# Attention and feed-forward kernel: scores of a pair of heads by 64-row tiles in two PSUM banks

## The chip, the cores and the metric

The kernel runs on one core of one Trainium2 chip. The metric is the device time of one execution in microseconds; lower is better.

## The reference

```python
# x: (16, 256, 128) float32
xn = layernorm(x)                                    # no scale, no shift
# attention: 16 heads of 8 dimensions
q = (xn @ Wq + bq);  latent = xn @ Wl + bl           # latent: 32 wide
k = latent @ Wk + bk;  v = latent @ Wv + bv          # each reshaped to (B, S, 16, 8)
scores = einsum('bihd,bjhd->bhij', q, k) * 8 ** -0.5
attn = softmax(scores, axis=-1)
a = einsum('bhij,bjhd->bihd', attn, v).reshape(B, S, 128) @ Wo + bo
# feed-forward: product keys, 8 heads, query of 2 x 16, 32 keys on each side
f = xn @ fWq + fbq                                   # (B, S, 8, 32), batch norm over it
s0, s1 = scores of the normalised halves against the two sets of normalised keys
top 4 of each side, the 16 sums of them, softmax -> w; the index of a sum picks an expert
eh = gelu(down[idx] . xn) * w;  m = sum of up[idx] * eh
out = x + a + m
```

## The kernel before, in words

The 16 sequences of 256 tokens make T = 4096 tokens. A first stage handles them in 8 chunks of 512 tokens (NC = 8): layer norm on DVE and ACT, transposes on PE, and the projections. Each of q and k is split into three bfloat16 parts (`parts`), spilled to DRAM (`spill`, on SP's queue) and read back (`load`) into QS and KS, in an order that makes one matmul over 48 rows (6 products of parts x 8 dimensions, `ROWS`) the exact score of one head. Head e of a pair (e = 0, 1) lies on partitions 64*e to 64*e+47, and rows 64*e+48 and 49 of QS take minus the row maximum of each query in two parts (`max_rows`, four DMAs per sequence) against rows of ones in KS. QS has one copy for each head of a pair: in the copy of head e the rows of the other head are zero, so a matmul over all 128 rows sees one head alone. The zeros and the ones are written by POOL at the very start, with a memset of QS (`qzero`) and one of KS (`kone`); SP waits for both before the first spill.

The main stage has 128 slots, one for each pair of heads of each sequence (n = 8*b + pr), and a further 17 slots in which the pipeline empties. A sequence, eight slots, is called a batch here, and k = slot % 8. The order of the work on each engine is written out by hand as a loop over slots, and the engines meet only through semaphores:

- PE in slot s: `si`, the scores of pair s with queries on partitions, two matmuls for each head (L506, bf16, 256 columns each), one PSUM bank for each head; `SJ`, the transposed scores minus the maximum of pair s-11 (LAG = 11), four matmuls over 128 rows (L565) into one of two 1024-wide buffers; in even slots or odd ones the product of exponentials and values (L587). From slot 10 on, head 0 of `si` stands ahead of SJ and head 1 behind it. In slots 1 to 9 both heads are issued together.
- DVE in slot s: the row maximum of each head, one 512-wide reduction for each (L844), which frees the bank for the next slot.
- ACT in slot s: the exponential of a whole SJ buffer (L404), and copies out of PSUM.
- Around these, by k, stands the feed-forward part of the batch: at k=0 DVE splits the maxima into two bf16 parts (L825, L827, `mpart`), and PE transposes them (L599); at k=1 and 2 PE makes the key scores (L611, called fs), ACT copies them, and DVE takes the top 8 at k=2 and 3 (L867, MAX8); POOL works from k=4 on a chain of small operations on them that ends with two large products (L1016) and one sum (L1024) at k=6 and 7; PE multiplies with these at k=3 (L627), collects the attention output at k=5 (L638), transposes it at k=6 (L645) and makes the output at k=7 (L652, L653).

The lines at the start that the prediction speaks of: L718 and L722 (layer norm statistics), L725 (variance plus epsilon, a TENSOR_SCALAR on 128x4) and L711 (normalising, TENSOR_SCALAR on 128x128) on DVE, L446 (the first transposes) on PE, which also waits for the constants and for fWq (L219), and L915 to L919 (the memsets) on POOL. L941, in slot 8 on POOL, adds the output bias to all of x. L549, on PE in slot 11, and L855, on DVE in slot 12, turn norms.

## Time and profile before

| | us |
|---|---|
| median of 3 runs | 505.98 |
| the three runs | 506.55, 505.98, 501.67 |
| span of the profiled execution | 500.5 |

The span goes from the first to the last instruction of one profiled execution. Which of the three runs was profiled isn't told; what lies around the span is between 1.2 and 6.1 us. Engines are PE (TensorE matmul), PEld (its weight loads), DVE (VectorE), ACT (ScalarE), POOL (GpSimd) and SP (the queue that issues the DMAs, SPq). Matmuls are pipelined and their ends are modelled: a matmul of 107 ns of streaming shows a duration of some 280 ns, and overlapping ones are merged in a timeline, so the step from one start to the next tells what a group costs. PEclk is the granted TensorE clock, 1.00 for 2.4 GHz and 0.50 for 1.2 GHz.

### The profile page before, as it was taken

The page shows a single profiled execution, that of the slowest core. Times are in us where ns is not written, and L with a number is a line of the kernel's source. Part 1 is how long each engine was busy: PE and PEld are TensorE (multiplying, and loading weights), DVE is VectorE, ACT ScalarE, POOL GpSimd, SP SyncE. Part 2 cuts the span into 40 slices and gives each one's busy share as a digit, 9 for nine tenths or more (in the row PEclk, how much of TensorE's full clock was granted, in tenths as well). Part 3 has the DMA queues.
Part 4 walks back from the last instruction along what each step waited for, and adds up shares of the span by engine and source line. Part 5 has one row for each costly group of instructions (what it writes and reads, how often), then busy time and mean ns, then how long its engine had stood idle before and what let it go on. Part 6 is the DMA issues. An engine that isn't in the chain of part 4 may idle for free.

```text
span 500.5 us, 10238 instructions
## 1 busy us (share of the span) xinstructions
PE 430.4 (86%) x3276; PEld 247.5 (49%) x3276; DVE 419.2 (84%) x1622; ACT 257.2 (51%) x387; POOL 291.3 (58%) x495
## 2 busy tenths in 40 slices
PE   0488768865799999999999999999999999999886
PEld 0353434331336465555556464656555564646554
DVE  6958659999789898888898898989888888989651
ACT  1265528761555555445555555555555555555560
POOL 9502016675295665849494756658494947566670
PEclk9999959996669999898999999999989899999997
DMA  7100583542814031231402040312304030000000
GB/s 208 23 1 1 114 107 96 136 127 55 105 24 65 15 52 47 32 63 15 75 2 77 3 76 22 55 49 29 68 9 75 3 77 3 10 14 1 24 0 22
DMA packets 45821, 24.79 MB, mean 50 GB/s; under 512 B 5384, under 2 KB 45640, under 8 KB 45768
## 3 DMA queue, kind: packets, MB, share of 16 engines
q1 hardware_dynamic: 45768, 24.14, 24.5%
q8 instruction: 26, 0.43, 0.4%
q14 instruction: 27, 0.22, 0.2%
HBM read 15.47 MB, written 8.39 MB: 48 GB/s over the span
## 4 chain that ended last, share of the span: by engine, by line
PE 57%; DVE 15%; issue 3%; POOL 3%; DMA 1%; POOLq 1%; SPq 0%; ACT 0%; DVEq 0%
PE bank L506 13%; PE SJ L565 11%; PE bank L587 9%; PE bank L611 6%; PE bank L627 6%; PE bank L638 5%; DVE mpart L827 4%; DVE negm L844 3%; DVE mpart L825 2%; PE bank L645 2%; DVE parts L686 2%; PE bank L652 2%; PE bank L653 1%; DVE r_sb L876 1%; DMA QS<-mT 1%
## 5 line engine op out<-in xcount | busy, mean ns | idle before, releaser
L844 DVE TENSOR_REDUCE negm<-bank 128x2 f32<-128x512 f32 x256 | 169.3, 683 | 32.2 <-PE bank L506 30.6
L404 ACT ACTIVATE Eb<-SJ 128x1024 f32<-128x1024 f32 x128 | 130.9, 1023 | 100.4 <-PE SJ L565 100.1
L506 PE MATMUL bank<-KS,QS 48*128 48x256 bf16 x512 | 99.1, 284 | 13.8 <-DVE negm L844 9.2
L565 PE MATMUL SJ<-QS,KS 128*128 128x256 bf16 x512 | 80.6, 282 | 0.4 <-DMA QS<-mT 0.4
L587 PE MATMUL bank<-Eb,vhat 128*32 128x256 f32 x1024 | 73.1, 406 | 0.0
L949 POOL COPY top<-top 128x32 f32<-128x32 f32 x32 | 6.7, 209 | 111.6 <-DVE top L867 111.6
L506 PEld LDWEIGHTS bank<-KS,QS 48*128 48x128 bf16 x512 | 27.6, 95 | 69.3 <-issue 33.4
L1016 POOL TENSOR_TENSOR prod<-r_sb,a 128x1024 f32<-128x1024 f32 x31 | 59.6, 1943 | 0.0
L565 PEld LDWEIGHTS SJ<-QS,KS 128*128 128x128 bf16 x512 | 41.1, 99 | 31.1 <-issue 26.0
L927 POOL TENSOR_TENSOR Eb<-Eb,parts 128x512 f32<-128x512 f32 x16 | 20.4, 1289 | 57.9 <-ACT parts L294 57.9
L867 DVE MAX8 top<-s_sb 128x8 f32<-128x32 f32 x512 | 50.5, 176 | 3.5 <-ACT s_sb L378 3.5
L876 DVE MATCH_REPLACE8 r_sb<-top,s_sb 128x36 f32<-128x36 f32 x256 | 42.7, 179 | 0.0
L587 PEld LDWEIGHTS bank<-Eb,vhat 128*32 128x32 f32 x1024 | 27.7, 113 | 26.9 <-issue 16.7
L611 PE MATMUL bank<-kblk,fqT 128*128 128x256 f32 x128 | 38.1, 422 | 0.1
L1024 POOL TENSOR_TENSOR prod<-prod 128x1024 f32<-128x1024 f32 x15 | 35.2, 2348 | 1.2
L627 PE MATMUL bank<-cst,prod 128*128 128x128 f32 x256 | 32.8, 281 | 2.2 <-DVE ysb L816 2.2
L387 ACT ACTIVATE Osb<-bank 128x256 f32<-128x256 f32 x64 | 24.1, 376 | 19.0 <-PE bank L587 19.0
L378 ACT ACTIVATE s_sb<-bank 128x512 f32<-128x512 f32 x32 | 19.1, 597 | 28.3 <-PE bank L611 28.3
L627 PEld LDWEIGHTS bank<-cst,prod 128*128 128x128 f32 x256 | 29.8, 191 | 5.8 <-issue 3.2
L638 PE MATMUL bank<-cst,Osb 128*128 128x36 f32 x256 | 31.5, 280 | 0.6 <-ACT Osb L387 0.6
L638 PEld LDWEIGHTS bank<-cst,Osb 128*128 128x128 f32 x256 | 29.8, 191 | 4.3 <-issue 4.3
L611 PEld LDWEIGHTS bank<-kblk,fqT 128*128 128x128 f32 x128 | 22.7, 197 | 12.3 <-issue 9.5
(149 smaller groups left out, 671.5 us busy)
## 6 DMA issues: line engine op xcount, KB each, us to landing
qk_parts<-parts SPq DMA_DIRECT2D x48, 128.0 KB, 2.4
QS<-qk_parts SPq DMA_DIRECT2D x32, 96.0 KB
KS<-qk_parts SPq DMA_DIRECT2D x32, 96.0 KB
x_sb<-L_attn_x SPq DMA_DIRECT2D x8, 256.0 KB, 3.7
QS<-qk_parts SPq DMA_DIRECT2D x32, 64.0 KB
KS<-qk_parts SPq DMA_DIRECT2D x32, 64.0 KB
out<-ysb SPq DMA_DIRECT2D x16, 128.0 KB, 3.9
QS<-qk_parts SPq DMA_DIRECT2D x32, 32.0 KB
```

Source lines behind the costliest of these rows:

```text
L404: A(Eb[:, n % 4, :], SJ[n % 2][:, :], ACT.Exp).then_inc(s["ex"], 1)
L506: last = mm(SI[e][:, t * S:(t + 1) * S], QS[r, b % RING, e, pr, t * P:(t + 1) * P], KS[r, b % RING, pr, :], start=True, stop=True)
L565: last = mm(SJ[n % 2][:, (e * BT + t) * S:(e * BT + t + 1) * S], KS[:, b % RING, pr, t * P:(t + 1) * P], QS[:, b % RING, e, pr, :], start= ...
L587: last = mm(psO[32 * c:32 * c + 32, (g % 2) * S:(g % 2 + 1) * S], vhat[:, v0:v0 + 32], Eb[:, (2 * g + c // 2) % 4, e0:e0 + S], start=(t == ...
L611: last = mm(psM[:, 256 * r:256 * (r + 1)], fqT[:, r, tok:tok + P], kblk[:, :, :].rearrange("p g k -> p (g k)"), start=True, stop=True)
L627: last = mm(psM[:, t * P:(t + 1) * P], prod[:, t, h, :, :].rearrange("p i j -> p (i j)"), ident, start=(h == 0), stop=(h == FH // 2 - 1))
L638: last = mm(ct[:, :, 2 * g * VC:2 * (g + 1) * VC], Osb[:, g, t * P:(t + 1) * P], sel, start=True, stop=True)
L844: V.tensor_reduce(negm[:, bb % 2, e, :, pr], SI[e].rearrange("p (t j) -> p t j", j=S), axis=AX, op=ALU.max, negate=True).then_inc(s["mx"], 1)
L867: last = V.max(top8[:, h, a, :], s_sb[:, h, a, 0:NK])
L876: last = V.match_replace(r_sb[:, h, :], top4[:, h, :], s_sb[:, h, 1, :], NEG)
L1016: TT(prod[:, t, :, :, :], r_sb[:, hs, 0:NK].unsqueeze(2).to_broadcast([P, FH, TOP, NK]), a0[:, hs, :].unsqueeze(3).to_broadcast([P, FH, TO ...
L1024: TT(prod[:, :, 0:FH // 2, :, :].rearrange("p t h i j -> p t (h i j)"), prod[:, :, 0:FH // 2, :, :].rearrange("p t h i j -> p t (h i j)"), ...
```

## The change

Both heads of a pair are now computed by matmuls on row tiles, head 0 on rows 0 to 47 (or 49) and head 1 on rows 64 to 111 (or 113), issued in turn (head inside, half of the queries or keys outside), and head e writes into bank e of a two-bank buffer. SI gets two such buffers; the second is used from slot 11 on (`FIRST2` = 10; up to slot 10 all slots use the first). SJ keeps one. QS has one copy, without zeros. All four matmuls of `si` stand ahead of SJ in every slot. The maxima of both heads are one 1024-wide reduction, and its semaphore counts slots and no longer heads. SJ of pair n waits for the exponential of pair n-1 (before: n-2). Both memsets are gone; the rows of ones come by two DMAs from 64 more columns of `const`, queued on SP behind the weight loads, and SP doesn't wait for them; PE does before the first SJ. PSUM buffers of the first stage are placed anew.

```diff
--- before.py
+++ after.py
@@ -30,7 +30,8 @@
 
 
 C_ID, C_SEL, C_AVG, C_GRP = 0, 128, 164, 292
-C_END = C_GRP + 248
+C_ONE = C_GRP + 248
+C_END = C_ONE + 64
 
 
 def constants():
@@ -42,6 +43,7 @@
             c[32 * col + r, C_SEL + 18 * (col % 2) + 9 * (col // 2) + r] = 1.0
     c[:, C_AVG:C_AVG + P] = (p[:, None] % 32 == p[None, :] % 32) / 8.0
     c[p, C_GRP + 120 + p // 16] = 1.0
+    c[:, C_ONE:C_END] = np.array([0x3F803F80], np.uint32).view(np.float32)
     return c
 
 
@@ -119,7 +121,7 @@
         bnv = sb("bnv", [P, 16])
         fqT = sb("fqT", [P, 2, T])
         rn_t = sb("rn_t", [P, CH]); rn = sb("rn", [P, NT, G])
-        QS = sb("QS", [P, RING, 2, NPAIR, S], BF16)
+        QS = sb("QS", [P, RING, NPAIR, S], BF16)
         KS = sb("KS", [P, RING, NPAIR, S], BF16)
         negm = sb("negm", [P, 2, 2, BT, NPAIR])
         mpart = sb("mpart", [P, BT, 2, 2, NPAIR], BF16)
@@ -146,22 +148,26 @@
         prod = sb("prod", [P, BT, FH, TOP, NK])
         wgT = sb("wgT", [P, S])
 
-        bank = [ctx.enter_context(nc.psum_tensor(f"bank{i}", [P, 512], F32)) for i in range(4)]
-        SJ = [ctx.enter_context(nc.psum_tensor(f"SJ{i}", [P, 1024], F32)) for i in range(2)]
-        SI = [bank[0][:, :], bank[1][:, :]]
-        psO, psM = bank[2][:, :], bank[3][:, :]
-
-        psX = [psO, SJ[1][:, 512:1024]]
-        psQ, psK, psV = SJ[0][:, 0:512], SJ[0][:, 512:1024], SJ[1][:, 0:512]
+        SI = [ctx.enter_context(nc.psum_tensor(f"SI{i}", [P, 1024], F32)) for i in range(2)]
+        SJ = ctx.enter_context(nc.psum_tensor("SJ", [P, 1024], F32))
+        bank = [ctx.enter_context(nc.psum_tensor(f"bank{i}", [P, 512], F32)) for i in range(2)]
+        psO, psM = bank[0][:, :], bank[1][:, :]
+
+        psX = [psO, SI[1][:, 512:1024]]
+        psQ, psK, psV = SJ[:, 0:512], SJ[:, 512:1024], SI[1][:, 0:512]
         psW = psQ
-        psF = [SI, [psM, psV]]
+        psF = [[SI[0][:, 0:512], SI[0][:, 512:1024]], [psM, psV]]
         psN = psO
-        psG = [psM, SJ[1][:, 512:1024]]
+        psG = [psM, SI[1][:, 512:1024]]
+        FIRST2 = NC + 2
+
+        def si_buffer(n):
+            return SI[n % 2] if n >= FIRST2 else SI[0]
 
 
         names = (
 
-            "w0 w w2 stats aggr var std rstd nm xn xn2 xT xnT vone kone qzero pad identb "
+            "w0 w w2 stats aggr var std rstd nm xn xn2 xT xnT vone kone pad identb "
 
             "wl wl_ev wkv wkv_ev q q_ev k k_ev v v_ev f f_ev f_st "
 
@@ -222,6 +228,11 @@
                         sp.dma_start(dst, src).then_inc(s["w"], 16)
             for dst, src in W2LOADS:
                 sp.dma_start(dst, src).then_inc(s["w2"], 16)
+            for e in range(2):
+                r0 = 64 * e + ROWS
+                ones = KS[r0:r0 + 2, :, :, :].rearrange("p a r n -> p (a r n)").bitcast(F32)
+                sp.dma_start(ones.rearrange("p (a n) -> p a n", n=64),
+                             const[0:2, C_ONE:C_END].unsqueeze(1).to_broadcast([2, RING * NPAIR * S // 128, 64])).then_inc(s["kone"], 16)
 
             def spill(c):
 
@@ -241,7 +252,7 @@
                 if b >= RING:
                     sp.wait_ge(s["sj"], NPAIR * (b - RING + 1))
                 for e in range(2):
-                    for t, dst in ((0, QS[:, b % RING, e]), (1, KS[:, b % RING])):
+                    for t, dst in ((0, QS[:, b % RING]), (1, KS[:, b % RING])):
                         for term, part, length in RUNS[t]:
                             r0 = 64 * e + DH * term
                             src = scratch[t, c, NPAIR * e:NPAIR * (e + 1), part:part + length].rearrange("r a d n -> (a d) r n")
@@ -254,10 +265,8 @@
                     for part in range(2):
                         src = (e * 2 + part) * NPAIR
                         r0 = 64 * e + ROWS + part
-                        sp.dma_start(QS[r0:r0 + 1, b % RING, e, :, :], mT[src:src + NPAIR, :]).then_inc(s["mrow"], 16)
-
-            sp.wait_ge(s["kone"], 1)
-            sp.wait_ge(s["qzero"], 1)
+                        sp.dma_start(QS[r0:r0 + 1, b % RING, :, :], mT[src:src + NPAIR, :]).then_inc(s["mrow"], 16)
+
             spill(0)
             load(0)
             load(1)
@@ -401,7 +410,7 @@
                     elif n == 0:
                         act.wait_ge(s["lo_q"], NC)
                         act.wait_ge(s["lo_k"], NC)
-                    A(Eb[:, n % 4, :], SJ[n % 2][:, :], ACT.Exp).then_inc(s["ex"], 1)
+                    A(Eb[:, n % 4, :], SJ[:, :], ACT.Exp).then_inc(s["ex"], 1)
                 if slot == NC + 2:
                     act.wait_ge(s["n2r"], NC // 2)
                     A(rn_t[:, :], rn_t[:, :], ACT.Sqrt).then_inc(s["n2s"], 1)
@@ -491,21 +500,26 @@
                 last.then_inc(s["bb"], 1)
                 pe.wait_ge(s["bc"], 1)
 
-            def si(n, heads):
+            def si(n):
 
                 b, pr = n // NPAIR, n % NPAIR
-                if pr == 0 and 0 in heads:
+                if pr == 0:
                     pe.wait_ge(s_load[b % RING], 16 * NLOAD * (b // RING + 1))
-                for e in heads:
-                    if n >= 1:
-                        pe.wait_ge(s["mx"], 2 * (n - 1) + e + 1)
-                    else:
-                        pe.wait_ge(s["f_ev"], 2 * NC)
-                    r = slice(64 * e, 64 * e + ROWS)
-                    for t in range(BT):
-                        last = mm(SI[e][:, t * S:(t + 1) * S], QS[r, b % RING, e, pr, t * P:(t + 1) * P],
-                                  KS[r, b % RING, pr, :], start=True, stop=True)
-                    last.then_inc(s["si"], 1)
+                if n == 0:
+                    pe.wait_ge(s["f_ev"], 2 * NC)
+                elif n <= FIRST2:
+                    pe.wait_ge(s["mx"], n)
+                elif n == FIRST2 + 1:
+                    pe.wait_ge(s["v_ev"], NC)
+                    pe.wait_ge(s["g_ev"], NC)
+                else:
+                    pe.wait_ge(s["mx"], n - 1)
+                for t in range(BT):
+                    for e in range(2):
+                        r = slice(64 * e, 64 * e + ROWS)
+                        last = mm(si_buffer(n)[:, (e * BT + t) * S:(e * BT + t + 1) * S],
+                                  QS[r, b % RING, pr, t * P:(t + 1) * P], KS[r, b % RING, pr, :], start=True, stop=True)
+                last.then_inc(s["si"], 1)
 
             def norms(c):
 
@@ -530,7 +544,7 @@
                     bn_mean()
                 if slot < NPAIR * B:
 
-                    si(slot, (0,) if slot > NC + 1 else (0, 1))
+                    si(slot)
                 if slot == 0:
                     bn_variance()
                 if 1 <= slot <= NC:
@@ -554,20 +568,19 @@
                     b, pr = n // NPAIR, n % NPAIR
                     if pr == 0:
                         pe.wait_ge(s["mrow"], 64 * (b + 1))
-                    if n >= 2:
-                        pe.wait_ge(s["ex"], n - 1)
+                    if n >= 1:
+                        pe.wait_ge(s["ex"], n)
                     else:
+                        pe.wait_ge(s["kone"], 32)
+                        pe.wait_ge(s["q_ev"], NC)
                         pe.wait_ge(s["k_ev"], NC)
-                        pe.wait_ge(s["v_ev"], NC)
-                        pe.wait_ge(s["g_ev"], NC)
-                    for e in range(2):
-                        for t in range(BT):
-                            last = mm(SJ[n % 2][:, (e * BT + t) * S:(e * BT + t + 1) * S],
-                                      KS[:, b % RING, pr, t * P:(t + 1) * P],
-                                      QS[:, b % RING, e, pr, :], start=True, stop=True)
+                    for t in range(BT):
+                        for e in range(2):
+                            r = slice(64 * e, 64 * e + ROWS + 2)
+                            last = mm(SJ[:, (e * BT + t) * S:(e * BT + t + 1) * S],
+                                      KS[r, b % RING, pr, t * P:(t + 1) * P],
+                                      QS[r, b % RING, pr, :], start=True, stop=True)
                     last.then_inc(s["sj"], 1)
-                if NC + 1 < slot < NPAIR * B:
-                    si(slot, (1,))
                 m = slot - LAG - 3
                 if m >= 0 and m % 2 == 0 and m // 2 < 4 * B:
 
@@ -818,7 +831,7 @@
                 b = slot // 8 - 1
                 if k == 0 and 0 <= b < B:
 
-                    dve.wait_ge(s["mx"], 2 * NPAIR * (b + 1))
+                    dve.wait_ge(s["mx"], NPAIR * (b + 1))
                     if b >= 1:
                         dve.wait_ge(s["mt"], b)
                     src = negm[:, b % 2, :, :, :].rearrange("p e t r -> p t e r")
@@ -839,10 +852,10 @@
                     q_ev(slot + 1)
                 if slot < NPAIR * B:
                     bb, pr = slot // NPAIR, slot % NPAIR
-                    for e in range(2):
-                        dve.wait_ge(s["si"], 2 * slot + e + 1)
-                        V.tensor_reduce(negm[:, bb % 2, e, :, pr], SI[e].rearrange("p (t j) -> p t j", j=S),
-                                        axis=AX, op=ALU.max, negate=True).then_inc(s["mx"], 1)
+                    dve.wait_ge(s["si"], slot + 1)
+                    V.tensor_reduce(negm[:, bb % 2, :, :, pr].rearrange("p e t -> p (e t)"),
+                                    si_buffer(slot)[:, :].rearrange("p (t j) -> p t j", j=S),
+                                    axis=AX, op=ALU.max, negate=True).then_inc(s["mx"], 1)
                 if 1 <= slot < NC - 1:
                     k_ev(slot + 1)
                 if 1 <= slot < NC:
@@ -913,8 +926,6 @@
             V = nc.gpsimd
             TT = V.tensor_tensor
             V.memset(vhat[:, :], 1.0).then_inc(s["vone"], 1)
-            V.memset(QS[:, :, :, :, :].rearrange("p c e r n -> p (c e r n)").bitcast(mybir.dt.uint32), 0).then_inc(s["qzero"], 1)
-            V.memset(KS[:, :, :, :].rearrange("p a r n -> p (a r n)"), 1.0).then_inc(s["kone"], 1)
             V.memset(s_sb[:, :, :, NK:KP], NEG)
             V.memset(top4[:, :, TOP:8], NEG).then_inc(s["pad"], 1)
 

```

## Rows read from the trace of the kernel before

**Rows 1.** The page, part 5: the costliest groups.

```profile
L844 DVE TENSOR_REDUCE negm<-bank 128x2 f32<-128x512 f32 x256 | 169.3, 683 | 32.2 <-PE bank L506 30.6
L404 ACT ACTIVATE Eb<-SJ 128x1024 f32<-128x1024 f32 x128 | 130.9, 1023 | 100.4 <-PE SJ L565 100.1
...
L587 PE MATMUL bank<-Eb,vhat 128*32 128x256 f32 x1024 | 73.1, 406 | 0.0
```

**Rows 2.** Timeline, first 21 us: start, duration, engine, line, count [idle before].

```profile
2.30 0.43 SPq L219 DMA_DIRECT2D fwq_sb<-L_ffn_Wq  x1
...
4.62 6.93 POOL L916 MEMSET QS<- 128x8192 uint32 x1
...
4.95 6.62 DVE L725 TENSOR_SCALAR ve<-mv 128x4 f32<-128x4 f32 x1
...
11.48 6.95 POOL L917 MEMSET KS<- 128x8192 bf16 x1
...
12.13 6.44 DVE L711 TENSOR_SCALAR Eb<-x_sb,mv,rs 128x128 f32<-128x128 f32 x2
...
18.72 2.05 PE L446 MATMUL bank<-cst,Eb 128*128 128x128 f32 x8 [18.72 <-DVE Eb L711]
...
19.80 0.17 DVE L725 TENSOR_SCALAR ve<-mv 128x4 f32<-128x4 f32 x1
...
20.53 0.59 DVE L711 TENSOR_SCALAR Eb<-x_sb,mv,rs 128x128 f32<-128x128 f32 x2
```

**Rows 3.** DMA issues of the first 20 us: size, us to landing.

```profile
fwq_sb<-L_ffn_Wq SPq DMA_DIRECT2D x1, 128.0 KB, 4.8
```

**Rows 4.** Timeline of PE, slot 3, both heads issued together.

```profile
78.55 0.40 PE L506 MATMUL bank<-KS,QS 48*128 48x256 bf16 x4
```

**Rows 5.** Timeline of PE in one steady batch, and L599 of the last.

```profile
283.67 0.29 PE L599 MATMUL bank<-ident_b,mpart 128*32 128x128 bf16 x2 [0.90 <-DVE mpart L827]
...
285.46 1.13 PE L611 MATMUL bank<-kblk,fqT 128*128 128x256 f32 x4
...
289.77 0.39 PE L506 MATMUL bank<-KS,QS 48*128 48x256 bf16 x2
290.09 0.61 PE L565 MATMUL SJ<-QS,KS 128*128 128x256 bf16 x4
...
290.95 2.05 PE L627 MATMUL bank<-cst,prod 128*128 128x128 f32 x16
...
466.83 0.28 PE L599 MATMUL bank<-ident_b,mpart 128*32 128x128 bf16 x2 [1.66 <-DVE mpart L827]
```

**Rows 6.** The tile negm: ns min/median/max, first and last start.

```profile
L827 DVE TENSOR_TENSOR mpart<-negm,mpart x14: 191/1845/1849, 167.2 to 464.9; 128x32 bf16<-128x32 f32 x14
```

**Rows 7.** Timeline of DVE and POOL around one steady batch.

```profile
283.54 1.87 DVE L844 TENSOR_REDUCE negm<-bank 128x2 f32<-128x512 f32 x3
...
291.67 1.57 DVE L867 MAX8 top<-s_sb 128x8 f32<-128x32 f32 x16
...
302.60 3.78 POOL L1016 TENSOR_TENSOR prod<-r_sb,a 128x1024 f32<-128x1024 f32 x2
...
303.76 0.78 DVE L825 CAST mpart<-negm 128x32 bf16<-128x32 f32 x1
...
304.58 1.85 DVE L827 TENSOR_TENSOR mpart<-negm,mpart 128x32 bf16<-128x32 f32 x1
```

**Rows 8.** Timeline of PE and DVE between slots 8 and 11.

```profile
122.34 2.07 PE L611 MATMUL bank<-kblk,fqT 128*128 128x256 f32 x4
...
131.15 0.69 DVE L844 TENSOR_REDUCE negm<-bank 128x2 f32<-128x512 f32 x1 [2.70 <-PE bank L506]
```

**Rows 9.** Windows: length, busy us by engine (count), PEclk, DMA share, GB/s.

```profile
131.70:135.10 3.40, 1.71 (x12) 0.64 (x10) 3.40 (x23) 1.18 (x2) 0.21 (x1) 1.00 1.00 100
135.10:145.30 10.20, 8.18 (x50) 2.88 (x52) 8.88 (x45) 5.07 (x6) 9.08 (x24) 0.50 0.46 54
148.00:205.00 57.00, 54.54 (x458) 31.84 (x457) 51.62 (x236) 30.89 (x43) 35.95 (x72) 1.00 0.28 46
```

## The prediction, made before the change was run

> **What bounds the kernel now.** I read the page first, then the timeline of the first 20 us, then one steady batch (eight slots) engine by engine, and last the granted clock of stretches. The page says that the maxima on DVE sat 30.6 us in all behind the score matmuls [rows 1], and in a steady stretch of 57 us PE was busy 54.5 [rows 9]. Shares don't say where an end is set, so the run is taken in parts.
>
> *The first 20 us* belong to POOL. Its memset of QS (6.93 us) and the one of KS (6.95 us) run back to back, and two small DVE operations last exactly until each ends: L725 takes 6.62 us where its next execution takes 0.17, and the pair at L711 takes 6.44 us where the next pair takes 0.59. The first matmul starts at 18.72 only because it waits for L711 [rows 2].
>
> *The steady part* is 14 batches; L827 runs once in each, 13 intervals from 167.2 to 464.9 us, so a batch takes 22.90 us [rows 6]. PE is the engine that never rests: in slot k=3 the order is scores of head 0 at 289.77, transposed scores at 290.09, head 1 behind them, next work at 290.95, which makes 1.18 us per slot for this block; it idles 0.90 us once, in front of L599 [rows 5]. A second limit lies just under it. L825 and L827, on 128x32 elements, take 0.78 and 1.85 us, and L827 ends at 306.43, with POOL's two products (302.60 + 3.78 = 306.38); I read this as DVE and POOL excluding one another. From the end of the second MAX8 group (291.67 + 1.57 = 293.24) to the end of L827 (306.43) is 13.2 us, stretch A, nearly all of it a chain of POOL operations. From the first maximum behind L827 (283.54) to 293.24 is 9.7 us, stretch B, which PE sets [rows 7]. A + B is the batch.
>
> *Between them*, slots 8 to 16, DVE once waits 2.70 us for the second head's scores, which stand behind transposed scores and other work in PE's order [rows 8].
>
> **The change part by part.**
>
> *Memsets gone.* DVE gains 6.62 - 0.17 = 6.45 us and 6.44 - 0.59 = 5.85 us, 12.3 us in a row [rows 2]. What is late next: the first matmul also waits for fWq, issued at 2.30 and landing 4.8 us later, at 7.1 us [rows 2, 3]; that would leave 18.72 - 7.2 = 11.5 us. The later chunks hang on DVE and ACT more than on this one start. Ends 11.5 and 12.3; I take 12.0. Everything behind is a chain on the same chunks, so the shift is kept to the end. The waits on kone and qzero leave SP; two DMAs that write the ones are queued on SP behind all weight loads, some 0.5 us of issue each as for other loads there, long before the first spill needs the queue: nothing. Their cost if that cover were gone is that 1 us.
>
> *Row tiles.* The trace has this operation already: in the early slots, where both heads are issued together, four L506 matmuls last 0.40 us [rows 4], while two of one head last 0.39 [rows 5]. The two heads run side by side. So scores and transposed scores, eight matmuls in four rounds of 0.11 us, need 0.44 us plus about 0.11 for the turn to other work: 0.55 us in place of 1.18. Ends: 0.55, and 0.98 if the second set (50 rows) did not overlap. I take 0.55, the near row. PE's work per batch falls by 8 x 0.63 = 5.0 us. The Trainium skill (TensorEngine Tiling (Array Packing), Tiling Modes, Key Properties) says that a change of tiling mode drains TensorE; both sets are now of one mode, and with a drain between them all the same the block would be 0.66 us, 0.9 us more per batch.
>
> *One maximum of 1024.* Three maxima in a row take 1.87 us, 0.62 each [rows 7]; two hold two fixed parts, the new one holds one. Between 1.13 (one fixed part of some 0.09 us less) and 1.25 us; I take 1.18, so 0.5 us less per batch. With two SI buffers the maximum no longer waits behind PE's slot.
>
> *SJ with one buffer.* Transposed scores now wait for the exponential of the slot before. That loop is 1.02 us of ACT [rows 1], 0.22 of matmuls and three hand-overs, taken at 0.2 each: 1.9 us, under a slot's 2.6 (an eighth of 21). In PE's queue behind the wait stand the value matmuls (L587), the feed-forward groups and the next slot's scores, for which DVE waits. Ends 0 and 0.4 us per slot (3.2 per batch); I take 0, since 1.9 is under 2.6.
>
> *Stretch B.* DVE's own work is four maxima (4.7 us) and two MAX8 groups (3.1): 7.9 us. PE's path is L599 0.4 (0.29 and a wait), block 0.55, L611 1.06 (a 1.13 us row with 0.07 of tail), block 0.55, the values 1.0 (73.1 us over 64 groups is 1.14 [rows 1], with tail), L611 1.06, scores 0.3, then one maximum and one MAX8 group: 7.7 us. So B is 7.9 where the clock is full.
>
> *Stretch A* does not shrink. DVE gains some 0.3 us in it (four maxima at 0.06), but POOL's chain is as long as before, and L825 and L827 wait for POOL's products again: 13.2. The batch would be 21.1 us.
>
> *But the clock.* PE's work is now 22.9 - 0.9 - 0.3 - 5.0 = 16.7 us in a batch of 21.1. Stretch B leaves it nearly no pause, so most of the 4.4 us left falls in A, over 3 of them in front of L599, which waits for L827; it idled 0.90 there before [rows 5]. The granted clock was 1.00 (2.4 GHz) over 57 us in which PE was busy 54.5; in the stretch from 131.7 to 135.1 PE was busy 1.71 of 3.4 us, and the 10.2 us behind it were granted 0.50 (1.2 GHz) [rows 9]. I expect this at the head of each batch, just where PE's path decides B. The fs block then takes 2.07 us in place of 1.06 [rows 5, 8]. Half clock for 3.4 us costs that path 1.7 us: 7.7 + 1.7 = 9.4. If it holds for 6.8 us it is 3.4 of the 5 us of PE's part: 11.1. Ends 7.9 and 11.1; part of a slow stretch falls into the idle time, so I take the middle, 9.5. The batch is 22.7 us, 0.2 less than now: 14 x 0.2 = 3 us. The Trainium skill (TensorE: Matmul & The Clock Gate, Part 1) says that throttled is the default and activity releases it; by that rule as by rows 9 a faster PE that must wait is punished for it.
>
> *Slots 8 to 16.* The 2.70 us wait goes, since both heads stand ahead of the transposed scores; PE is at half clock there in both. Ends 0 and 2.9; I take 2.5. POOL's long addition in slot 8 stays.
>
> *Tail.* No maxima are left, POOL's chain sets it: 0.
>
> *Sum.* 12.0 + 2.5 + 3 = 17.5 us. The profiled execution has a span of 500.5; the runs shown are 501.67 to 506.55, so between 1 and 6 us lie around it, and I cannot say which run it was. The steps are differences, so they are set against the median: 505.98 - 17.5 = 488.
>
> **The rivals.**
>
> *The clock holds* (or the slow stretches fall where PE has slack). For: before the last L599 PE idled 1.66 us [rows 5] and ran on at 2.4 GHz. Against: 3.3 us is twice that. Batch 21.1: 505.98 - 14.5 - 14 x 1.8 = 466.
>
> *DVE gets in first.* L825 starts at 303.76, 1.16 us behind POOL's products [rows 7]. Some 0.4 of that is a wait for PE's output, 0.2 one for the second head at k=7, and the shorter maxima give 0.3: about 0.25 is left, within the error of my count. If it gets in, one product (1.9 us) [rows 7] no longer stands between it and L827, A is 11.3 and the idle time of PE is about 1.5 us. Batch 19.2 to 20.9, so 28 to 52 us more than the head's gain: 440 to 463, 455 as its figure. Against: both chains start with the same MAX8 end, and nothing makes POOL's longer.
>
> *Slower: PE stays at half clock.* If PE falls at the start of each batch and the single SJ buffer keeps it too thinly fed to recover, B goes to 11.1 and A, where PE's 12 us become about 20, grows as well. The place is L611 in slots k=1 and 2, then L627 and L638. At 11.1 + 13.2 = 24.3 the loss is 14 x 1.4 = 20 us, more than the 14.5 gained before; with 0.5 more in A it is 513. It decides from a batch of 22.90 + 14.5/14 = 23.9 us. Against: slow stretches in the trace end when PE has had a full load.
>
> *It doesn't do what it says:* the head's 12 us are taken up by another wait (loads, the spill queue), or the 50-row tiles don't overlap. Then 498 to 502.
>
> **How the numbers follow.** Forecast 488 (482 to 498): 0.53. Clock holds, 466: 0.20. DVE first, 455: 0.12. Slower, 513: 0.07. Gain taken up, 500: 0.08. A measurement of this kernel tells about 1% from no change, 501 to 511 us. Faster: all of the first three and a third of the last, 0.88; within 1%: the rest of the last and an edge of the slow case, 0.06; slower 0.06. The range for 8 in 10 takes in "clock holds" and the middle of "DVE first", and leaves out most of the slow case: 455 to 501.
>
> **What would show it.** L725 at 0.17 us and the first matmul near 7 us show the head's step; anything above 9 us shows it wrong. The eight matmuls of a slot within 0.55 us show the row tiles. L844 at 1.13 to 1.25 us x128. L827 still ending with POOL's second product, 13.2 us behind the second MAX8 group, shows A; an L827 of 0.2 us would show the race won. An idle time of about 3 us before L599 with PEclk below 9 in most slices of the steady part shows the clock; PEclk at 9 throughout with a batch of 21 us, or a batch above 23.9, would make the forecast wrong.

## The result, and the profile after

The changed kernel takes 458.77 us (median of 4 runs, 454.42 to 462.76) beside 503.83 us (497.40 to 506.55) of the kernel before on the same chip: a ratio of 0.912, 95% interval 0.904 to 0.920. The ratios leave out slow runs, those over 1.5% above the fastest of their kernel, such as the 462.76 us here. By the medians it is 45 us faster, where 17.5 us were forecast. Its profiled execution has a span of 456.2 us (before 500.5), so 44.3 us are to be found. The granted clock's mean over the span is 0.929 of full, before 0.938.

The page of the kernel after, its parts 1, 2 and 5 (answering [rows 1]):

```profile
PE 357.8 (78%) x3276; PEld 219.6 (48%) x3276; DVE 402.0 (88%) x1494; ACT 254.6 (56%) x387; POOL 275.8 (60%) x493
...
PEclk9989789875689899999999999999999898999897
...
L413 ACT ACTIVATE Eb<-SJ 128x1024 f32<-128x1024 f32 x128 | 131.1, 1024 | 55.5 <-PE SJ L580 52.3
L856 DVE TENSOR_REDUCE negm<-SI 128x4 f32<-128x1024 f32 x128 | 153.7, 1209 | 9.3 <-PE SI L520 8.7
L600 PE MATMUL bank<-Eb,vhat 128*32 128x256 f32 x1024 | 72.0, 401 | 0.0
...
L612 PE MATMUL bank<-ident_b,mpart 128*32 128x128 bf16 x32 | 5.0, 242 | 45.6 <-DVE mpart L840 45.6
```

DVE now waits 8.7 us for scores in the whole run (before 30.6), and PE's largest idle time is in front of L612, 45.6 us. Half clock is rare: PEclk reads 9 through the middle of the run, which the forecast named as what would make it wrong. (Lines have moved: L725, L711, L446, L599, L611, L627, L844, L825, L827 are now L738, L724, L455, L612, L624, L640, L856, L838, L840, and L506, L565, L587, L867, L1016 are L520, L580, L600, L880, L1027.)

The timeline of its first 10 us (answering [rows 2]):

```profile
4.78 0.17 DVE L738 TENSOR_SCALAR ve<-mv 128x4 f32<-128x4 f32 x1
...
5.51 0.60 DVE L724 TENSOR_SCALAR Eb<-x_sb,mv,rs 128x128 f32<-128x128 f32 x2
...
6.75 2.07 PE L455 MATMUL bank<-cst,Eb 128*128 128x128 f32 x8 [6.75 <-DMA fwq_sb<-L_ffn_Wq]
```

L738 lasts 0.17 us where its twin lasted 6.62, and the first matmul starts at 6.75, released by the load of fWq: 12.0 us earlier.

The timeline of one steady batch, PE, DVE and POOL in turn (answering [rows 5, 7]; a number in brackets is the idle time ahead):

```profile
240.07 0.39 PE L520 MATMUL SI<-KS,QS 48*128 48x256 bf16 x4
240.30 0.38 PE L580 MATMUL SJ<-QS,KS 50*128 50x256 bf16 x4
240.61 1.07 PE L600 MATMUL bank<-Eb,vhat 128*32 128x256 f32 x16
...
253.32 0.28 PE L612 MATMUL bank<-ident_b,mpart 128*32 128x128 bf16 x2 [2.90 <-DVE mpart L840]
...
254.08 1.13 PE L624 MATMUL bank<-kblk,fqT 128*128 128x256 f32 x4
...
239.89 0.55 DVE L880 MAX8 top<-s_sb 128x8 f32<-128x32 f32 x5
...
249.89 1.50 DVE L838 CAST mpart<-negm 128x32 bf16<-128x32 f32 x1
251.42 1.84 DVE L840 TENSOR_TENSOR mpart<-negm,mpart 128x32 bf16<-128x32 f32 x1
253.19 3.62 DVE L856 TENSOR_REDUCE negm<-SI 128x4 f32<-128x1024 f32 x3
...
259.33 1.58 DVE L880 MAX8 top<-s_sb 128x8 f32<-128x32 f32 x16
...
249.44 3.78 POOL L1027 TENSOR_TENSOR prod<-r_sb,a 128x1024 f32<-128x1024 f32 x2
```

Eight score matmuls take 240.61 - 240.07 = 0.54 us, counted from their first start to the next group's. L838 starts 0.45 us behind POOL's products and L840 ends with them (253.26 beside 253.22). The second MAX8 group of the batch before (its end is the first of the DVE lines) ends at 239.89 + 0.55 = 240.44, so stretch A is 253.26 - 240.44 = 12.8 us; this batch's second group ends at 260.91, so stretch B is 7.7 us. Together 20.5.

The tile mpart of the kernel after (ns min/median/max, first and last start), answering [rows 6]:

```profile
L838 DVE CAST mpart<-negm x16: 167/1500/1582, 106.7 to 417.1; 128x32 bf16<-128x32 f32 x16
L840 DVE TENSOR_TENSOR mpart<-negm,mpart x16: 191/1843/1845, 106.9 to 418.7; 128x32 bf16<-128x32 f32 x16
```

The starts of the cast in either trace cut the run into four parts:

| part | before | after | difference | forecast |
|---|---|---|---|---|
| start to the first cast | 120.16 | 106.68 | -13.5 | -12.0 |
| first to second cast (slots 8 to 16) | 23.90 | 19.26 | -4.6 | -2.5 |
| 14 batches behind it | 320.1 | 291.2 | -28.9 | -3 |
| last cast to end | 36.4 | 39.06 | +2.7 | 0 |

So 29 of the 44 us were won where 3 had been forecast: 22.86 us per batch became 20.80. Eleven of the 14 batches take 19.95 to 20.9 us, three 22.0. A stretch at half clock starts in each of those three; the first of the 14 also catches the end of an earlier one. In the kernel before four such stretches start in its 14 batches. The mean granted clock over the 14 batches is 0.98 in both kernels.

Windows of the kernel after (length, busy us of PE, PEld, DVE, ACT and POOL with counts, PEclk, DMA share, GB/s): the pause ahead of L612 and what follows it, in a batch that takes 22.0 us, then in one that takes 20.5, then in another of 22.0, and at last the tail's slow stretch:

```profile
146.00:149.40 3.40, 0.50 (x10) 0.09 (x2) 3.37 (x3) 0.48 (x1) 3.32 (x3) 1.00 0.00 0
149.40:152.80 3.40, 3.40 (x18) 1.80 (x20) 2.12 (x2) 1.78 (x4) 2.46 (x2) 0.50 0.01 3
249.90:253.30 3.40, 0.52 (x12) 0.04 (x4) 3.37 (x4) 0.58 (x1) 3.32 (x3) 1.00 0.02 5
253.30:256.70 3.40, 3.38 (x39) 1.84 (x39) 3.35 (x3) 3.02 (x5) 2.58 (x2) 1.00 0.01 2
...
374.70:378.10 3.40, 0.53 (x12) 0.05 (x4) 3.37 (x4) 0.59 (x1) 3.33 (x2) 1.00 0.00 0
378.10:381.50 3.40, 3.37 (x16) 1.81 (x18) 2.24 (x2) 1.66 (x3) 2.58 (x2) 0.50 0.01 2
...
442.90:446.30 3.40, 3.40 (x16) 3.29 (x16) 0.00 (x0) 0.00 (x0) 0.00 (x0) 0.51 0.17 43
```

PE does the same half microsecond of work in each of the three pauses. Behind the first and the third the granted clock is 0.50 (1.2 GHz) for 3.4 us; behind the second it stays at 2.4 GHz. What decides between them these rows don't show.

### The profile page after: what moved, and what is told of

Read it like the earlier page. It is cut to its first block, busy times and chain, and to the rows that moved or that the text cites. A ratio compares the mean times of both kernels' runs of the same rounds, so it can differ in the third digit from the quotient of the medians.

```text
span 456.2 us, 10109 instructions
## 1 busy us (share of the span) xinstructions
PE 357.8 (78%) x3276; PEld 219.6 (48%) x3276; DVE 402.0 (88%) x1494; ACT 254.6 (56%) x387; POOL 275.8 (60%) x493
## 4 chain that ended last, share of the span: by engine, by line
DVE 39%; issue 15%; POOL 14%; PE 10%; POOLq 1%; DMA 1%; SPq 0%; ACT 0%; DVEq 0%
DVE negm L856 12%; DVE r_sb L889 6%; DVE top L880 6%; DVE mpart L840 4%; PE bank L624 3%; DVE mpart L838 3%; POOL prod L1035 3%; POOL prod L1027 2%; DVE parts L699 2%; PE SI L520 2%; PE bank L640 2%; POOL z_sb L977 1%; POOL rank L997 1%; DVE ysb L829 1%; POOL cmp L987 1%
## 5 line engine op out<-in xcount | busy, mean ns | idle before, releaser
L413 ACT ACTIVATE Eb<-SJ 128x1024 f32<-128x1024 f32 x128 | 131.1, 1024 | 55.5 <-PE SJ L580 52.3
L856 DVE TENSOR_REDUCE negm<-SI 128x4 f32<-128x1024 f32 x128 | 153.7, 1209 | 9.3 <-PE SI L520 8.7
L600 PE MATMUL bank<-Eb,vhat 128*32 128x256 f32 x1024 | 72.0, 401 | 0.0
L1027 POOL TENSOR_TENSOR prod<-r_sb,a 128x1024 f32<-128x1024 f32 x31 | 59.5, 1941 | 0.0
L520 PE MATMUL SI<-KS,QS 48*128 48x256 bf16 x512 | 53.3, 289 | 6.7 <-DVE negm L856 3.8
L580 PE MATMUL SJ<-QS,KS 50*128 50x256 bf16 x512 | 51.4, 280 | 5.1 <-ACT Eb L413 4.2
L880 DVE MAX8 top<-s_sb 128x8 f32<-128x32 f32 x512 | 50.4, 176 | 5.1 <-ACT s_sb L387 5.1
L624 PE MATMUL bank<-kblk,fqT 128*128 128x256 f32 x128 | 40.8, 446 | 0.3
L612 PE MATMUL bank<-ident_b,mpart 128*32 128x128 bf16 x32 | 5.0, 242 | 45.6 <-DVE mpart L840 45.6
L600 PEld LDWEIGHTS bank<-Eb,vhat 128*32 128x32 f32 x1024 | 27.4, 112 | 26.4 <-issue 16.1
L640 PE MATMUL bank<-cst,prod 128*128 128x128 f32 x256 | 34.0, 289 | 6.1 <-ACT s_sb L387 3.3
L640 PEld LDWEIGHTS bank<-cst,prod 128*128 128x128 f32 x256 | 31.3, 200 | 10.3 <-issue 6.7
L378 ACT ACTIVATE mT<-bank 32x256 bf16<-32x256 f32 x16 | 6.0, 373 | 50.2 <-PE bank L612 50.2
L387 ACT ACTIVATE s_sb<-bank 128x512 f32<-128x512 f32 x32 | 19.1, 597 | 23.7 <-PE bank L624 23.3
L520 PEld LDWEIGHTS SI<-KS,QS 48*128 48x128 bf16 x512 | 15.3, 96 | 35.4 <-issue 22.1
L624 PEld LDWEIGHTS bank<-kblk,fqT 128*128 128x128 f32 x128 | 24.1, 210 | 14.2 <-issue 8.6
```

The costliest lines, as they stand in the source:

```text
L413: A(Eb[:, n % 4, :], SJ[:, :], ACT.Exp).then_inc(s["ex"], 1)
L520: last = mm(si_buffer(n)[:, (e * BT + t) * S:(e * BT + t + 1) * S], QS[r, b % RING, pr, t * P:(t + 1) * P], KS[r, b % RING, pr, :], start= ...
L580: last = mm(SJ[:, (e * BT + t) * S:(e * BT + t + 1) * S], KS[r, b % RING, pr, t * P:(t + 1) * P], QS[r, b % RING, pr, :], start=True, stop ...
L600: last = mm(psO[32 * c:32 * c + 32, (g % 2) * S:(g % 2 + 1) * S], vhat[:, v0:v0 + 32], Eb[:, (2 * g + c // 2) % 4, e0:e0 + S], start=(t == ...
L624: last = mm(psM[:, 256 * r:256 * (r + 1)], fqT[:, r, tok:tok + P], kblk[:, :, :].rearrange("p g k -> p (g k)"), start=True, stop=True)
L640: last = mm(psM[:, t * P:(t + 1) * P], prod[:, t, h, :, :].rearrange("p i j -> p (i j)"), ident, start=(h == 0), stop=(h == FH // 2 - 1))
```

## The experiments

Theory after the result: the work itself costs 20.5 us per batch, and the clock decides how much of that is seen; PE's 2.9 us pause is a state in which it may fall. Rivals: the gain is one part of the change (second SI buffer, wide maximum, the memsets), and the clock only fills idle time.

**One part undone at a time, and one made alone.** First both memsets back on POOL, with SP waiting for them, and without the DMAs of ones.

```diff
-                sp.dma_start(ones.rearrange("p (a n) -> p a n", n=64),
...
+            V.memset(QS[:, :, :, :].rearrange("p c r n -> p (c r n)"), 0.0).then_inc(s["qzero"], 1)
+            V.memset(KS[:, :, :, :].rearrange("p a r n -> p (a r n)"), 1.0).then_inc(s["kone"], 1)
```

> The changed kernel with both memsets back on POOL at the start (8192 elements each, as long as before), SP waiting for them, and no DMAs of ones. Theory (the head's gain is two DVE operations that no longer wait for a memset, and it is kept to the end): L738 takes 6.6 us and the first L724 pair 6.4 again, the first matmul starts near 18.7 us, and the time is 12 to 13.5 us above the changed kernel, some 471 to 473 us. Rival (the head's gain is made good elsewhere, in loads or in the spill queue, and the whole gain is in the main stage): under 465 us.

Measured 483.25 us (ratio 0.948, 0.938 to 0.958), 24.5 above the changed kernel. The first cast starts at 119.09, 12.4 us later, as expected, but the time is above the expected 471 to 473. In the profiled execution (span 478.2) the other 9.6 us lie behind the first cast: 8 of its 14 batches take 21.1 to 23.4 us, the others 20.2 to 20.5. The four runs lie far apart, 475.76 to 486.45 us.

Then the kernel before with the scores of both heads ahead of SJ.

```diff
-                    si(slot, (0,) if slot > NC + 1 else (0, 1))
+                    si(slot, (0, 1))
...
-                if NC + 1 < slot < NPAIR * B:
-                    si(slot, (1,))
```

> The kernel before with one edit in PE's order: all four score matmuls stand ahead of the transposed scores in every slot, as they do up to slot 9. Still one bank for each head, 512-wide maxima, memsets, 128-row transposed scores. Theory (PE's order sets the batch): the block takes 0.33 + 0.54 = 0.87 us in place of 1.18, PE's batch is 2.5 us shorter, but head 1 now waits for its maximum ahead of the transposed scores, which gives back part: batch 21.5 to 22.4 us against 22.9, time 490 to 500 us. Rival (the second SI buffer is what pays, since the maxima's wait is the bound): no change or slower, batch 22.9 or more.

Measured 505.44 us (ratio 1.0006, 0.9972 to 1.004): nothing. Two batches without a slow stretch take 22.16 us and one 21.4, where such a batch of before takes 22.8 as a rule; the other 11 hold a slow stretch and take 23.7. So it looks as if the gain was there and the clock took it back; no run has this order with the clock held up, so that is not shown.

The changed kernel with one SI buffer, and with one SI and two SJ:

```diff
-        FIRST2 = NC + 2
+        FIRST2 = NPAIR * B
```

> The changed kernel with FIRST2 set so high that all scores go through one SI buffer of two banks. Theory (DVE and POOL set the batch now, PE has slack): each maximum waits 0.4 to 0.5 us for matmuls that can only start when the maximum before has ended; in the stretch of slots k=0 to 3 nothing hides this (1.5 us), in the POOL-bound stretch the wait of L838 for POOL's first product hides it: batch 22 us against 20.5, time 478 to 485 us. Rival (the row tiles alone bring the gain, the buffer nothing): within 3 us of the changed kernel.

> The changed kernel with the PSUM map the other way round: one two-bank buffer for the scores (SI) and two for the transposed scores (SJ), each transposed set waiting for the exponential of two slots before. Against e3 it differs by the second SJ buffer alone. Theory (one SJ buffer costs nothing, since its loop is shorter than a slot): as e3, batch 22 to 24 us, time 495 to 501 us. Rival (the single SJ buffer costs up to 0.4 us per slot): 3 us per batch less than e3, time below 470 us.

Measured 499.43 us (497.89 to 501.16) and 498.86 us (496.45 to 499.16). The first is above its expected range. With one SI buffer, a second SJ buffer is worth nothing: both have batches of 23.9 us, and both have the slow stretches. Whether it would be worth something with two SI buffers no run shows, but the trace of the changed kernel speaks against it: in its 14 batches PE never waits for an exponential in front of L580. Timeline and windows of the one-SI kernel around L612, in one batch:

```profile
291.15 0.39 PE L612 MATMUL bank<-ident_b,mpart 128*32 128x128 bf16 x2 [1.91 <-DVE mpart L840]
```

```profile
287.50:290.90 3.40, 1.61 (x24) 0.78 (x24) 3.37 (x3) 1.02 (x1) 3.40 (x2) 1.00 0.00 0
290.90:297.70 6.80, 5.81 (x38) 2.76 (x38) 4.35 (x11) 3.28 (x5) 2.71 (x3) 0.50 0.05 13
297.70:314.80 17.10, 13.57 (x152) 9.05 (x144) 16.22 (x72) 8.83 (x12) 12.03 (x27) 1.00 0.33 51
```

From the second batch on each repeats this: 6.8 us at half clock, 17.1 at full. Stretch B takes 11.1 us here, the upper end that the prediction gave it. This is its slow case, with 23.9 us per batch, its deciding point.

The changed kernel with two 512-wide maxima per slot:

```diff
+                    for e in range(2):
+                        last = V.tensor_reduce(negm[:, bb % 2, e, :, pr],
+                                               si_buffer(slot)[:, 512 * e:512 * (e + 1)].rearrange("p (t j) -> p t j", j=S),
+                                               axis=AX, op=ALU.max, negate=True)
+                    last.then_inc(s["mx"], 1)
```

> The changed kernel with two 512-wide maxima per slot (they still wait for both heads together and free the buffer together). Theory (DVE's fixed part is 0.08 us each, and DVE's path is one of two equal ones behind L840): batch up by 0.2 to 0.4 us, to 20.7 to 20.9 us, time 1 to 8 us above the changed kernel, clock falls apart. Rival (the wide maximum is a main part of the gain): more than 10 us above it.

Measured 482.16 us (480.66 to 486.02), 23 us worse: far above expectation. From the second batch on they take 22.3 or 23.6 us, with half clock in each. Each of the three undone versions lost more than was expected of the edit itself.

**The clock taken out.** Three matmuls of no use go into the pause, from the third batch on; they write a bank that the next transposes overwrite, and wait for nothing that L612's slot did not already wait for.

```diff
+                    if b >= 2:
+                        pe.wait_ge(s["fin"], b - 1)
+                        for _ in range(3):
+                            mm(psM, ident, xnT[:, 0:CH], start=True, stop=True)
                     pe.wait_ge(s["ms"], b + 1)
...
-                    if b >= 2:
-                        pe.wait_ge(s["fin"], b - 1)
```

> The changed kernel with three more matmuls per batch from the third on, fp32 128x512, results unused, on PE in the pause in front of L612 (they wait for the output sum of the batch and not for the split maxima, and end about when L840 ends). Everything else is as in the changed kernel. Theory (the pause of 2.9 us is what lets the clock fall, in some executions in many batches and in others in few, at 1.5 us or more a time): PEclk stays at 1.00 through the steady part, every batch takes 20.5 us, mean granted clock above 0.95, and the time is 449 to 455 us, with runs closer together than those of the changed kernel. Rival (the falls have another cause, such as the low activity at L651): falls stay, time 457 to 463 us. Rival (PE is late for L612 because of the extra work): batch 20.7 us or more, time above 460 us.

Measured 452.75 us (449.40 to 455.46; ratio 0.9005, 0.8963 to 0.9047), 6 us less than the changed kernel by the medians, with more work. The two intervals touch (0.9036 and 0.9047), so of this pair alone only the batches of the traces speak clearly. Its timeline of PE at the same place, and its windows, in one fence each:

```profile
267.71 2.84 PE L609 MATMUL bank<-xnT,cst 128*128 128x512 f32 x6
270.70 0.29 PE L614 MATMUL bank<-ident_b,mpart 128*32 128x128 bf16 x2 [0.15 <-DVE mpart L842]
```

```profile
267.30:270.70 3.40, 3.25 (x18) 1.06 (x7) 3.37 (x4) 0.54 (x1) 3.32 (x3) 1.00 0.00 0
270.70:274.10 3.40, 3.40 (x39) 1.86 (x39) 3.35 (x4) 3.05 (x5) 2.56 (x2) 1.00 0.04 8
```

The three matmuls (recorded as six) fill 2.84 us and the pause is down to 0.15; the clock is 1.00 from 127 to 444 us, and the batches are 20.5 us but for one of 21.3. In the changed kernel three batches were 1.5 us longer and have lost it here. The same matmuls then went into each undone version:

> The changed kernel with one SI buffer (499.43 us so far, 23.9 us per batch with half clock for 6.8 us in each), now with three idle-time fp32 matmuls of 512 columns in the pause in front of the transposes of mpart, from the third batch on; each writes a bank that the next transposes overwrite, and no result changes. Theory (the second SI buffer is worth some 1 to 1.5 us per batch by itself, the rest of the loss is the half clock that its absence brings): no half-clock stretch in the steady part, a batch of 21.5 to 22.3 us, 466 to 478 us. Rival 1 (one SI buffer costs its 3 us per batch through waits alone, the half clock is only what the waits leave behind and covers idle time): the batch stays above 23.3 us with the clock at 1.00, 490 us or more. Rival 2 (the clock is all): 20.5 to 20.8 us per batch, 452 to 457 us.

> The changed kernel with two 512-wide maxima per slot (482.16 us so far, clock falls in every batch), now with the same three matmuls in the pause. Theory (the wide maximum saves only its fixed part on DVE, 0.04 us x 8 per batch, and the rest of the 23 us that its absence cost was clock): batch 20.7 to 20.9 us, 455 to 461 us. Rival (the second maximum lengthens the hand-over from PE to DVE and back in every slot): clock at 1.00 and a batch of 21.5 us or more, over 467 us.

> The changed kernel with both memsets back on POOL (483.25 us so far), now with the same three matmuls. Theory (the memsets cost 12.4 us in the head and nothing else; the other 12 us were half-clock stretches in the steady part of those executions): 452.75 + 12.4 = 465 us, 462 to 468. Rival (the memsets, or the missing DMAs of ones, cost time in the steady part too): 475 us or more, with a batch above 21 us at a clock of 1.00.

| kernel | us | same with the three matmuls | its usual batch there | cost of the edit by itself | what the clock added |
|---|---|---|---|---|---|
| changed | 458.77 | 452.75 | 20.49 | | 6.0 |
| one SI buffer | 499.43 | 466.43 (465.13 to 468.44) | 21.52 | 13.7 | 33.0 |
| two maxima | 482.16 | 458.88 (457.21 to 461.68) | 20.80 | 6.1 | 23.3 |
| memsets | 483.25 | 465.54 (463.10 to 468.22) | 20.48 | 12.8 | 17.7 |

The cost by itself is the third column's difference from 452.75; what the clock added is the second column less the third. The memsets' 17.7 is uncertain, because of the scatter of their runs: the two shorter ones, 475.76 and 480.11, would make it 12. The groups of runs were measured apart; the kernel before took 503.08 to 503.95 us beside them. All three times and batches lie where the theories put them and the rivals fall. One SI buffer keeps two stretches at half clock in its 14 batches, so its 13.7 us may hold a little of the clock's. The page of the one-SI kernel without and with the matmuls, its row of maxima:

```profile
L856 DVE TENSOR_REDUCE negm<-SI 128x4 f32<-128x1024 f32 x128 | 155.3, 1213 | 45.0 <-PE SI L520 44.8
```

```profile
L858 DVE TENSOR_REDUCE negm<-SI 128x4 f32<-128x1024 f32 x128 | 155.1, 1212 | 16.9 <-PE SI L520 16.6
```

The same buffers, the same order: DVE's wait for scores falls from 44.8 to 16.6 us with three matmuls added, and stretch B from 11.1 to 8.7. The second SI buffer is worth 1.03 us per batch. The wide maximum is worth 0.31: two maxima of 677 ns overlap and take 1.28 us from the first start to the last end, the one takes 1.21, which is at most 0.5 us in eight slots. The rest of their 33 and 23 us came with 1.2 GHz. Between a batch of before without a slow stretch (22.81) and 20.48 there remains 1 us for the row tiles and PE's order, if the parts add up; no run undoes the row tiles alone. The same three matmuls elsewhere in the batch were not tried, so that they must stand in this pause isn't shown.

**What bounds the batch then.** DVE's maximum ahead of L838, to see whether A shortens:

```diff
-                if k == 0 and 0 <= b < B:
...
-                    V.tensor_copy(mpart[:, :, :, 0, :], src).then_inc(s["mh"], 1)
...
                                     axis=AX, op=ALU.max, negate=True).then_inc(s["mx"], 1)
+                b = slot // 8 - 1
+                if k == 0 and 0 <= b < B:
...
+                    V.tensor_copy(mpart[:, :, :, 0, :], src).then_inc(s["mh"], 1)
```

> The changed kernel with one edit in DVE's order: at k=0 the maximum of the slot stands ahead of the split of the maxima (L838, L840). Theory (L838 and L840 wait for POOL's two products whenever they are issued, while a maximum, whose input is in PSUM, does not): L840 ends with the second product as before, the maximum is done inside that wait, the stretch from there to the second MAX8 group is 1.1 us shorter, batch 19.3 to 19.5 us, time 442 to 446 us. Rival (L838 and L840 are slow by themselves, or wait for something in DVE's own queue): the batch stays at 20.5 us.

Measured 469.79 us (468.38 to 471.16): worse. Timeline of one batch, all engines:

```profile
299.30 3.78 POOL L1028 TENSOR_TENSOR prod<-r_sb,a 128x1024 f32<-128x1024 f32 x2
...
299.75 1.22 DVE L847 TENSOR_REDUCE negm<-SI 128x4 f32<-128x1024 f32 x1
300.88 0.37 DVE L857 CAST mpart<-negm 128x32 bf16<-128x32 f32 x1
301.28 1.84 DVE L859 TENSOR_TENSOR mpart<-negm,mpart 128x32 bf16<-128x32 f32 x1
...
303.18 0.28 PE L612 MATMUL bank<-ident_b,mpart 128*32 128x128 bf16 x2 [2.90 <-DVE mpart L859]
...
303.83 1.23 DVE L847 TENSOR_REDUCE negm<-SI 128x4 f32<-128x1024 f32 x1 [0.71 <-PE SI L520]
...
305.44 1.23 DVE L847 TENSOR_REDUCE negm<-SI 128x4 f32<-128x1024 f32 x1 [0.38 <-PE SI L520]
```

The maximum runs beside POOL's products at no cost, so DVE has one less to do in B; but it then waits 0.71 and 0.38 us for PE. The batch without a slow stretch stays at 20.47, and B in it at 7.65 us, so PE's path and DVE's tie there. The order also brought more slow stretches: 9 of the 14 batches take 20.9 to 23.5 us.

Transposed scores twice, with the three matmuls in the pause:

```diff
-                    for t in range(BT):
+                    for t in list(range(BT)) * 2:
```

> The changed kernel with the three matmuls in the pause (452.75 us), and each slot's four transposed-score matmuls issued twice, the second time over the same result: 0.22 us more of PE's work per slot, 1.8 us per batch. Theory (with the clock full, PE's path and DVE's tie in stretch B, and A hangs on POOL): only the slots of stretch B count, so the batch grows by 0.4 to 0.7 us, 458 to 463 us. Rival 1 (PE's order bounds every slot): plus 1.8 us per batch, 476 us or more. Rival 2 (DVE alone bounds B): no change, 451 to 455 us.

Measured 462.46 us (456.84 to 464.74), a batch of 21.05. Of 8 x 0.22 = 1.8 us more work on PE, 0.56 show, all in B (8.22 beside 7.65 us); A stays at 12.84. PE's order counts in B and has slack elsewhere.

Both together: the maximum first, the three matmuls, SI of slots k=1 to 3 issued a slot earlier, and the second L624 group ahead of the values in k=2.

```diff
+                if slot >= 24 and k in (1, 2) and slot < NPAIR * B:
+                    si(slot + 1)
...
+                if k == 2:
+                    values()
```

> The filler matmuls, and the order of e4 on DVE (maximum of k=0 ahead of L838 and L840), and on PE from the third batch on: the scores of slots k=1, 2 and 3 stand one slot earlier (the first of them ahead of the wait for the split maxima), and at k=2 the second L624 group ahead of the values. Theory (behind L840 two equal paths, one on DVE and one on PE, set the stretch to the second MAX8 group, so that e4 alone, which shortened one, could gain nothing): both are shorter now, that stretch goes from 7.7 to about 7 us, batch 19.6 to 19.9 us, time 440 to 448 us. Rival (POOL's chain or something else sets the batch): batch 20.5 us and the time of the filler run alone.

Measured 448.43 us (447.41 to 453.24; ratio 0.8918, 0.8873 to 0.8962), the fastest here, with batches of 20.17. Its profiled execution, with a span of 451.4 us, is the longest of the six. The gain per batch is 0.3 us, less than expected (19.6 to 19.9). Timeline of DVE in one batch:

```profile
250.02 1.84 DVE L871 TENSOR_TENSOR mpart<-negm,mpart 128x32 bf16<-128x32 f32 x1
252.16 2.36 DVE L859 TENSOR_REDUCE negm<-SI 128x4 f32<-128x1024 f32 x2 [0.29 <-PE SI L520]
...
257.23 1.57 DVE L893 MAX8 top<-s_sb 128x8 f32<-128x32 f32 x16
259.10 0.42 DVE L823 TENSOR_TENSOR wgT<-bank,xnT 128x256 f32<-128x256 f32 x1 [0.30 <-PE bank L652]
```

B is 258.80 - 251.86 = 6.94 us, near the 7 expected, 0.7 less than without the new order. A has grown from 12.84 to 13.23: right behind B, DVE now waits 0.30 us for PE.

## Why the prediction came out as it did

**Where it held.** The head: 12.0 us at the first matmul, forecast 12.0, and 12.8 by experiment. The row tiles: 0.54 us for eight matmuls, forecast 0.55, with 48 and 50 rows alike. The wide maximum: 1.21 us, a little above the 1.18 taken, within its bounds. One SJ buffer at nothing: two buffers took 498.86 beside 499.43, with one SI buffer each; in the changed kernel's 14 batches PE doesn't wait for the exponential there, and its 4.2 us of such waits lie in slots 11 to 16 and the tail. Stretch A, tied to POOL's products: 12.8 us, forecast 13.2. Stretch B where the clock is full: 7.7 us, forecast 7.9. The pause ahead of L612: 2.90 us, forecast "over 3". Direction right, and the time inside the range of 455 to 501, near its lower end.

**The step that failed** is "But the clock". Its "Half clock for 3.4 us costs that path 1.7 us" was near in size (22.0 instead of 20.5, 1.5 us), but some half clock was charged to each of 14 batches. In the profiled execution three of the 14 took 1.5 us longer. So the term of B was 9.5 and the steady gain 3 us, where B was 7.65 in the batches without half clock and 9.1 to 9.2 in those with it, and the gain 28.9. Of the 26 us missed, about 18 are this step: 1.6 us per batch charged, 0.3 paid (3 x 1.5 over 14). The other 8 are sizes: A 0.4 and B 0.2 us shorter at full clock, 14 times. The prediction reasoned that a pause of over 3 us must lead to half clock as in [rows 9]; three pauses with the same half microsecond of work ended in 1.2, 2.4 and 1.2 GHz. The middle of the bounds 7.9 and 11.1 stood for something that is not a middle: in a batch it came whole or not at all. The rival "the clock holds" had the batch at 21.1 and 466 us, and was given 0.20; its mechanism is the nearest. The 455 us of "DVE gets in first" are nearer in number by luck, since that race was lost.

That the clock was the right thing to fear is shown by the undone versions: with one SI buffer, two maxima or the memsets, filling the pause at the same place gave back 33, 23 and 12 to 18 us, against 6 in the changed kernel. The Trainium skill (TensorE: Matmul & The Clock Gate, Part 1) has it that throttled is the default and activity releases it; the runs agree with it, since three useless matmuls per batch kept the granted clock at 1.00 for nearly all of the 14 batches and made each of the four kernels faster (by 1.3, 6.6, 4.8 and 3.7%, in the order of the table, the first of them near the scatter).

**Mis-sized terms.** Slots 8 to 16: 4.6 us, forecast 2.5 with an upper end of 2.9. DVE's timeline of the kernel before has three more waits for scores in that stretch beside the 2.70 us of [rows 8]:

```profile
124.99 1.29 DVE L844 TENSOR_REDUCE negm<-bank 128x2 f32<-128x512 f32 x2 [0.66 <-PE bank L506]
...
141.83 0.69 DVE L844 TENSOR_REDUCE negm<-bank 128x2 f32<-128x512 f32 x1 [0.44 <-PE bank L506]
...
143.34 0.69 DVE L844 TENSOR_REDUCE negm<-bank 128x2 f32<-128x512 f32 x1 [0.81 <-PE bank L506]
```

That is 4.61 us with the one counted; the kernel after has one of 0.71 us there. 3.9 us of waits and eight maxima shorter by some 0.06 make 4.4 of the 4.6. The forecast had priced one wait and taken it for all. The tail: +2.7 us where 0 was forecast. Two stretches at half clock lie in it (422.5 to 425.9, and the one at 442.9 shown above). In PE's timeline of the kernel after, beside the same group at full clock:

```profile
258.60 2.02 PE L640 MATMUL bank<-cst,prod 128*128 128x128 f32 x16 [0.23 <-ACT s_sb L387]
...
442.83 3.65 PE L640 MATMUL bank<-cst,prod 128*128 128x128 f32 x16 [1.63 <-DVE ysb L829]
```

That is 1.6 us. The filled kernel, whose clock is 1.00 up to 444 us, has a tail of 35.9 us, less than the 36.4 of before; so the tail's loss is the clock's, a term that the forecast left out there. The head gave 1.5 us more at the first cast than at the first matmul. That is partly scatter: in versions that are alike up to there (one SI buffer, and the changed kernel and the one-SI kernel with the three matmuls) the first cast starts at 105.0, 105.0 and 107.1. And with the memsets back it starts at 119.09, 1.1 us ahead of the kernel before. The slow case's figure of 513 us was also summed wrongly: its own terms give 511, and 518 with 0.5 us more per batch in A.

**The rivals.** "DVE gets in first": it lost, by 0.45 us where 0.25 was thought left, and in every batch of the trace from the third cast on. The slow case did not come for this kernel. Its mechanism, put on the single SJ buffer, was wrong: the version with two SJ and one SI buffer has it too, and the one with one SJ and two SI has not; it was the single SI buffer that brought 23.9. The head's gain was not taken up by another wait.

What stays open: what decides whether a given pause is followed by half clock. Pauses of 1.6 us (both heads together, in the kernel before) and 1.9 us (one SI) were followed by it in 11 and 13 of 14 batches, pauses of 2.9 us in three of 14 in the changed kernel, but pauses of 3.0 us in 13 of 14 with two maxima. So the length of the longest pause alone does not order the kernels.

## What to carry to other kernels

Cost an edit at full clock and the clock apart, because they don't add: small edits moved this kernel by 6 to 14 us in themselves and by 12 to 33 through TensorE's clock. Where PE has a pause of microseconds in each period, fill it with spare matmuls before comparing versions; the comparison then shows the edit, and here the kernel got faster too. And give a price that comes whole or not at all two cases with chances of their own, not a middle value.

## What was not expected of the hardware

The same pause, with PE busy 0.50 to 0.53 of 3.4 us, was followed by 1.2 GHz in two batches and by 2.4 GHz in another; the kernel with one SI buffer, with the same work and a shorter longest pause (1.9 us), fell in 13 of 14.

DVE and POOL exclude one another by operation, not always: beside POOL's products the cast and the subtraction on mpart stretch to 1.50 and 1.84 us, but the maximum that reads PSUM keeps its 1.22 us, as the batch with the maximum first shows. Unhindered, in the second batch of the changed kernel, they take (timeline of DVE):

```profile
125.94 0.18 DVE L838 CAST mpart<-negm 128x32 bf16<-128x32 f32 x1
126.16 0.22 DVE L840 TENSOR_TENSOR mpart<-negm,mpart 128x32 bf16<-128x32 f32 x1
```

The Trainium skill (SBUF — State Buffer, SBUF: two separate sides) says that the shared port pair is an exclusive lock, for DVE operations in a two-port mode, or with two SBUF inputs beside a GpSimd operation that reads SBUF. The traces agree: the maximum, with its one input in PSUM, isn't held up, while the subtraction with two SBUF inputs is. In the kernel before, the TENSOR_SCALAR on 4 columns beside a memset was held up too, for 6.45 us.
